# Causal attention: the third output tile of an even step is accumulated in the bank of the widest score tile

## The chip, the cores and the metric

The kernel runs on one core of one Trainium2 chip. Its time is the device time of one launch in microseconds (us). Work is spread over TensorE (PE in the profile, its weight loads PEld), VectorE (DVE), ScalarE (ACT), GpSimd (POOL) and SyncE (SP), which run their own instruction streams and wait for each other on semaphores.

## The reference

Two transformer layers on x of 4 x 512 x 512 (batch, time, width). The change lies in the first layer's attention, run on the layer-normed, modulated h:

```python
q = (x @ wq).reshape(B, T, H, HD)          # H = 32 heads of HD = 128
k, v = x @ wk, x @ wv                      # 8 groups, 4 query heads share one
q, k = rope(q), rope(k)
scores = einsum('bhtd,bhsd->bhts', q, k) / sqrt(HD)
att = softmax(where(causal, scores, -inf))
out = einsum('bhts,bhsd->bhtd', att, v)    # -> B, T, H*HD
return out @ wo                            # (T, 4096) @ (4096, 512)
```

After it come a feed-forward with sign weights, a second attention and a routed low-rank feed-forward; the change does not touch them.

## The kernel before

The batch of 4 is done in two halves of two. In each half `stage_groups` does the attention of the first layer: 64 steps n, one for each of 2 x 32 heads. Two heads make a pair p = n // 2. A float32 product is made of three matmuls on rounded parts (high x high, high x low, low x high), so a 128-row tile with 128 of contraction takes three matmuls.

In step n TensorE does, in this order: transpose the softmaxed scores of head n (`turn`, L713, 4 + 3 tiles), project a key or a value where one is due (`step_e(n, 1)`, L655), make the scores of head n+1 (`scores(n + 1)`, L677), project the query of head n+2 (L655), transpose the last 3 tiles; then in an **even** step three of the four output tiles of the pair before, `out_proj(4(p-1))`, `+1`, `+2` (L758); in an **odd** step probabilities times values, early and late part (`weigh_early`, `weigh_late`, L724), with the fourth tile, `+3`, between them. A key is projected in steps 1, 5, 9, ..., a value in steps 2, 6, 10, ... An output tile is six matmuls of 128 x 512: two heads by three part products. VectorE then adds the tile to a running sum in SBUF (`add`, L1006), and counts `w_added`. The running sum is `y` in the first half and `x` in the second.

PSUM has eight banks of 128 x 512, all taken: `pj` (projections), `pS0`, `pS1`, `pS2` (scores), `pT0`, `pT1` (transposes), `pO` and `pW`. `pS2` holds the widest score tile, of the last 128 rows by 512 keys; it is part 3 of `scores`, done last. VectorE reads the scores in `maxes` (L974), which counts `max_done`, four for each head; once it has read the widest tile, `pS2` is free. In odd steps `pS2` also takes the late half of probabilities times values. Output tiles alternate: first `pW`, second `pO`, third `pW`, fourth `pW`. So the third tile waits until the first has been added.

In an even step VectorE does, after the maxes and the softmax scaling of head n+1: the low part of the last transposes (`pt_los`, L982), the first add, the rounding of the rotated query to its high part (`rope_parts`, L963, which waits for GpSimd's rotation L1143, L1146), the second add, the third add. GpSimd then makes the query's low part `ql` (L1155), which the next step's `scores` needs before its fifth matmul. In the first half, from step 55 on, a piece of the modulation matrices is worked on between the second and the third output tile (`modulate`, L771, L783). After step 63 four more output tiles follow.

Of the kernel before, what the change touches and what calls it, by code (L numbers as in the profile page):

```python
# [27 lines left out]
TT = T // P  # L28
# [474 lines left out]
def stage_groups(nc, held, a, wts, half):  # L503
# [4 lines left out]
    with Stage(nc, f"gqa{half}") as st:  # L508
# [18 lines left out]
        pS = [st.ps(f"pS{i}", [P, T]) for i in range(3)]  # L527
        pT = [st.ps(f"pT{i}", [P, T]) for i in range(2)]
        pO, pW = st.ps("pO", [P, T]), st.ps("pW", [P, D])
# [6 lines left out]
        s_full, max_done, exp_done = st.sem("s_full"), st.sem("max_done"), st.sem("exp_done")  # L536
# [3 lines left out]
        w_full, w_added = st.sem("w_full"), st.sem("w_added")  # L540
# [18 lines left out]
        NTILES = NH // 2 * TT  # L559
# [4 lines left out]
        FIRST_ADDED = NTILES - 2 * TT  # L564

        def wbank(d):
            return pO if d % TT == 1 or d == NTILES - 1 else pW

        def split_no(what, i, group):

            return next(n for n, s in enumerate(SPLIT_LIST) if s[:3] == (what, i, group)) + 1
# [12 lines left out]
        with nc.Block() as block:  # L584
# [39 lines left out]
            def _(pe):  # L624
                def free(e):

                    kind, i = PROJ[e]
                    if kind == "V":
                        pe.wait_ge(v_out, i + 1)
                    else:  # L630
                        pe.wait_ge(cosed, ROPE.index(e) + 1)
# [36 lines left out]
                def scores(n):  # L668
                    u, r = n // R0, n % 2
                    q, k = PROJ.index(("Q", n)), PROJ.index(("K", u))  # L670

                    def part(i, parts):
                        s, c = S_AT[i]
                        t, wide = slice(i * P, (i + 1) * P), max((i + 1) * P, NARROW)
                        for m in parts:
                            qp, kp = ((qh, kh), (qh, kl), (ql, kh))[m]
                            mm = pe.matmul(pS[s][:, c:c + wide], qp[r][:, t], kp[u % 2][:, 0:wide], start=(m == 0), stop=(m == 2))  # L677
                        return mm

                    def drained(s):  # L680
                        if n:
                            pe.wait_ge(max_done, 4 * (n - 1) + S_MAXES[s])

                    pe.wait_ge(rope_hi, ROPE.index(q) + 1)
                    pe.wait_ge(rope_lo, ROPE.index(k) + 1)
                    drained(0)
                    part(1, (0, 1))
                    drained(1)
                    part(0, (0, 1))
                    pe.wait_ge(rope_lo, ROPE.index(q) + 1)  # L690
                    part(1, (2,)).then_inc(s_full, 1)
                    part(0, (2,))
                    part(2, (0, 1, 2)).then_inc(s_full, 1)
                    drained(2)
                    if n >= 3:
                        pe.wait_ge(o_lo, (n - 1) // 2 * 2)
                    part(3, (0, 1, 2)).then_inc(s_full, 1)

                def turn(n, jobs):
# [17 lines left out]
                def weigh(p, out, blocks):  # L717

                    u, m, last = 2 * p // R0, 0, 3 * len(blocks) - 1
                    for j, chunk, at, src, w in blocks:  # L720
                        pe.wait_ge(pt_lo, 3 * (2 * p + 1) + chunk + 1)
                        v = slice(j * P, (j + 1) * P)
                        for vp, pp in ((vh, pth), (vh, ptl), (vl, pth)):
                            mm = pe.matmul(out[:, :, at:at + w], vp[u % 2][:, v], pp[:, :, src:src + w], start=(m == 0), stop=(m == last))  # L724
                            m += 1
                    mm.then_inc(o_full, 1)
# [10 lines left out]
                def weigh_late(p):  # L737

                    pe.wait_ge(max_done, 4 * min(2 * p + 3, NH))
                    weigh(p, late, [(0, 0, 0, PT_OFF[0] + 2 * P, 2 * P), (1, 1, 0, PT_OFF[1] + P, 2 * P),  # L740
                                    (2, 2, 0, PT_OFF[2], 2 * P), (3, 2, P, PT_OFF[3], P)])

                def out_proj(d):

                    pair, i = d // TT, d % TT
                    if d == 0:
                        free(4)
                    if i == 0:
                        pe.wait_ge(o_lo, 2 * pair + 2)
                        pe.wait_ge(w_lo, split_no("o", (2 * pair + 1) % R0, pair // (R0 * HB // 2)))  # L750
                    before = [f for f in range(max(0, d - TT), d) if wbank(f) is wbank(d)]
                    if before:
                        pe.wait_ge(w_added, before[-1] + 1)
                    t = slice(i * P, (i + 1) * P)
                    m = 0
                    for h in (2 * pair, 2 * pair + 1):
                        for op, wp in ((oh, wts.oh), (oh, wts.ol), (ol, wts.oh)):
                            mm = pe.matmul(wbank(d)[:], op[pair % 2][:, h % 2, t], wp[:, h % R0, :], start=(m == 0), stop=(m == 5))  # L758
                            m += 1
                    mm.then_inc(w_full, 1)  # L760
# [25 lines left out]
                for e in range(4):  # L786
                    project(e)
                turn_values(0)
                scores(0)
                for n in range(NH):  # L790
                    if n == 0:
# [6 lines left out]
                    if n + 1 < NH:  # L798
                        scores(n + 1)
# [8 lines left out]
                    p = n // 2  # L808
                    if n % 2 == 0:
                        if p:  # L810
                            out_proj(TT * (p - 1))
                            out_proj(TT * (p - 1) + 1)
                        if later and n >= LATER_AT:
                            modulate(n - LATER_AT)
                        if p:
                            out_proj(TT * (p - 1) + 2)
                    else:
                        weigh_early(p)
                        if p:
                            out_proj(TT * (p - 1) + 3)  # L820
                        weigh_late(p)
                        if later and n >= LATER_AT:
                            modulate(n - LATER_AT)
# [112 lines left out]
            def _(dve):  # L936
# [64 lines left out]
                def add(d):  # L1001
                    dve.wait_ge(w_full, d + 1)
                    if d >= TT:
                        dve.wait_ge(w_added, d - TT + 1)
                    j = (d // (2 * TT)) % HB * TT + d % TT
                    nc.vector.tensor_tensor(y[:, j, :], wbank(d)[:], y[:, j, :], ALU.add).then_inc(w_added, 1)  # L1006
# [1054 lines left out]
```

## Time and profile before

| | us |
|---|---|
| three runs | 2176.83, 2180.11, 2181.4 (median 2180.11) |
| the profiled execution | 2177.08 |
| its span, first to last instruction | 2175.1 |
| mean granted TensorE clock in it | 0.957 of full speed |

The span is 2 us short of the profiled execution's own time. A row of the profile gives a group of instructions by source line, engine and the tiles that it writes and reads; busy time on TensorE is modelled, since its matmuls overlap, so distances between the starts of matmuls tell more than their durations. "Idle before" is the time for which an engine (or TensorE's weight loads, PEld) did nothing ahead of an instruction, with the one that released it.

### The profile page before, as it was taken

Reading aid. Unit: us, or ns where it says so; the run is one execution under the profiler, and the core shown is the slowest. Engines: PE = TensorE matmul, PEld = TensorE weight load, DVE = VectorE, ACT = ScalarE, POOL = GpSimd, SP = SyncE. Lnnn points to the kernel's source line nnn. Section 1 sums busy time; section 2 is a strip of 40 time slices with the busy share of each in tenths; the row PEclk is TensorE's granted clock in tenths of the full one; section 3 lists DMA queues with packets and bytes.
Section 4 is the critical chain, followed back from the end, with each engine's and each line's share of the span. In section 5 each row is a group of like instructions: output and inputs, shape, how many; then the busy total and the mean of one; then the engine's idle time right before and its main releaser. Section 6 shows DMA issues by size and latency. Waiting matters only on the chain. (4 is left out here: it accounts for less than half of the span.)

```text
span 2175.1 us, 33305 instructions
## 1 busy us (share of the span) xinstructions
PE 1987.6 (91%) x11441; PEld 1596.0 (73%) x11441; DVE 1483.2 (68%) x3679; ACT 1067.9 (49%) x2422; POOL 1039.8 (48%) x801
## 2 busy tenths in 40 slices
PE   4899999999999996897948999999999999978797
PEld 3788888888888774475527888888888888745664
DVE  4666676766767666966756767676676667779386
ACT  3555555555555552433235555555555555543232
POOL 3546564645646431544046555555555555417241
PEclk8999999999999997898969999999999999988899
DMA  5000101011010234146321101010110100041561
GB/s 171 20 30 20 30 20 30 20 30 49 20 30 20 78 107 139 64 101 129 85 95 41 30 12 38 20 30 20 30 49 8 42 20 1 30 141 39 116 123 39
DMA packets 132007, 115.30 MB, mean 53 GB/s; under 512 B 43201, under 2 KB 93441, under 8 KB 131841
## 3 DMA queue, kind: packets, MB, share of 16 engines
q1 hardware_dynamic: 124784, 105.51, 16.8%
q10 hardware_dynamic: 7056, 7.68, 1.2%
q8 instruction: 93, 1.52, 0.3%
q14 instruction: 74, 0.60, 0.1%
HBM read 92.15 MB, written 16.81 MB: 50 GB/s over the span
## 5 line engine op out<-in xcount | busy, mean ns | idle before, releaser
L860 ACT ACTIVATE gqa_prob<-gqa_prob,gqa_nmax 128x256 f32<-128x256 f32 (+3 forms) x512 | 284.2, 556 | 154.9 <-DVE gqa_nmax L974 146.6
L870 ACT CAST gqa_pth<-gqa_pT 128x384 fp32r<-128x384 f32 (+1 forms) x384 | 185.5, 519 | 205.3 <-PE gqa_pT L713 202.9
L974 DVE CUSTOM_DVE_ANT_0 gqa_prob<-gqa_pS,consts 128x256 f32<-128x256 f32 (+3 forms) x512 | 222.7, 486 | 58.9 <-PE gqa_pS L677 56.9
L1143 POOL TENSOR_TENSOR x<-x,consts 128x512 f32<-128x512 f32 x80 | 107.3, 1341 | 312.3 <-ACT x L844 312.3
L1143 POOL TENSOR_TENSOR y<-y,consts 128x512 f32<-128x512 f32 x80 | 107.3, 1342 | 303.1 <-ACT y L844 303.1
L982 DVE TENSOR_TENSOR gqa_ptl<-gqa_pT,gqa_pth 128x384 fp32r<-128x384 f32 (+1 forms) x384 | 217.2, 594 | 24.4 <-ACT gqa_pth L870 24.3
L713 PE MATMUL gqa_pT<-consts,gqa_prob 128*128 128x128 f32 x1280 | 183.8, 275 | 20.7 <-DVE gqa_ptl L982 19.2
L655 PE MATMUL gqa_pj<-first_hh,wqh 128*128 128x512 f32 x496 | 195.9, 395 | 0.0
L655 PE MATMUL gqa_pj<-first_hh,wql 128*128 128x512 f32 x496 | 194.7, 393 | 0.0
L655 PE MATMUL gqa_pj<-first_hl,wqh 128*128 128x512 f32 x496 | 194.1, 391 | 0.0
L713 PEld LDWEIGHTS gqa_pT<-consts,gqa_prob 128*128 128x128 f32 x1280 | 154.3, 141 | 48.8 <-DVE gqa_prob L998 15.1
L998 DVE TENSOR_SCALAR gqa_prob<-gqa_prob,gqa_rden 128x128 f32<-128x128 f32 (+3 forms) x512 | 186.4, 427 | 4.6
L758 PE MATMUL gqa_pW<-woh,gqa_oh 128*128 128x512 f32 x380 | 163.3, 430 | 9.7 <-DVE x L1006 5.3
L677 PE MATMUL gqa_pS<-gqa_kh,gqa_qh 128*128 128x256 f32 (+3 forms) x512 | 165.5, 334 | 0.0
L677 PE MATMUL gqa_pS<-gqa_kl,gqa_qh 128*128 128x256 f32 (+3 forms) x512 | 156.6, 324 | 0.0
L758 PE MATMUL gqa_pW<-wol,gqa_oh 128*128 128x512 f32 x380 | 151.0, 397 | 0.0
L758 PE MATMUL gqa_pW<-woh,gqa_ol 128*128 128x512 f32 x380 | 150.8, 397 | 0.0
L677 PE MATMUL gqa_pS<-gqa_kh,gqa_ql 128*128 128x256 f32 (+3 forms) x512 | 144.4, 323 | 1.3 <-POOL gqa_ql L1155 1.3
L655 PE MATMUL gqa_pj<-first_hh,wkvh 128*128 128x512 f32 x248 | 104.2, 420 | 22.3 <-PEq L83 22.3
L994 DVE RECIPROCAL gqa_rden<-gqa_den 128x4 f32<-128x4 f32 x128 | 22.8, 178 | 136.3 <-ACT gqa_prob L860 136.3
L877 ACT CAST gqa_oh<-gqa_pS 128x512 fp32r<-128x512 f32 x64 | 37.5, 586 | 147.3 <-PE gqa_pS L724 147.3
L655 PEld LDWEIGHTS gqa_pj<-first_hh,wqh 128*128 128x128 f32 x496 | 93.2, 188 | 20.6
(333 smaller groups left out, 5284.4 us busy)
## 6 DMA issues: line engine op xcount, KB each, us to landing
raw_o<-in_wo SPq DMA_DIRECT2D x16, 1024.0 KB, 5.2
raw_q<-in_wq SPq DMA_DIRECT2D x14, 1024.0 KB, 5.6
raw_q<-in_wmod SPq DMA_DIRECT2D x10, 1024.0 KB, 5.2
raw_kv<-in_wkv SPq DMA_DIRECT2D x14, 512.0 KB, 6.8
vp<-mid_hf SPq DMA_DIRECT2D x64, 64.0 KB, 1.8
kp<-mid_hf SPq DMA_DIRECT2D x16, 256.0 KB, 2.3
qp<-mid_hf SPq DMA_DIRECT2D x16, 256.0 KB, 2.5
tail_bd<-vp SPq DMA_DIRECT2D x64, 64.0 KB, 3.0
```

Of the source, the lines that this page charges most:

```text
L655: mm = pe.matmul(bank[e][:], wp, hp[:, k, t], start=(n == 0), stop=(n == 3 * KT - 1))
L677: mm = pe.matmul(pS[s][:, c:c + wide], qp[r][:, t], kp[u % 2][:, 0:wide], start=(m == 0), stop=(m == 2))
L713: mm = pe.transpose(pT[k % 2][:, c:c + P], prob[n % 2][:, P_OFF[i] + j * P:P_OFF[i] + (j + 1) * P], held.ident)
L758: mm = pe.matmul(wbank(d)[:], op[pair % 2][:, h % 2, t], wp[:, h % R0, :], start=(m == 0), stop=(m == 5))
L860: ins = nc.scalar.activation(p, p, ACT.Exp, scale=-1.0, bias=nmax[r][:, i:i + 1], accum_out=den[r][:, i:i + 1])
L870: nc.scalar.copy(pth[:, n % 2, c:c + w], pT[k % 2][:, 0:w]).then_inc(pt_hi, 1)
L877: nc.scalar.copy(oh[p % 2][:, :, part * HALF_T:(part + 1) * HALF_T], (early, late)[part]).then_inc(o_hi, 1)
L974: nc.vector.tensor_tensor_reduce(prob[r][:, P_OFF[i]:P_OFF[i] + w], pS[s][:, c:c + w], held.mask[:, T - w:T], -1.0, LARGEST, ALU.add, ALU.min,
L982: nc.vector.tensor_tensor(ptl[:, n % 2, c:c + w], pT[k % 2][:, 0:w], pth[:, n % 2, c:c + w].bitcast(F32), ALU.subtract).then_inc(pt_lo, 1)
L994: nc.vector.reciprocal(rden[n % 2][:], den[n % 2][:]).then_inc(recip, 1)
L998: ins = nc.vector.tensor_scalar(p, p, rden[n % 2][:, i:i + 1], None, ALU.mult)
L1143: nc.gpsimd.tensor_tensor(rot[r % 2][:], rot[r % 2][:], held.sinT, ALU.mult).then_inc(sined, 1)
```

## The change

The third output tile of an even step, all but the last pair's, is accumulated in `pS2` in place of `pW`. Three waits go with it. The tile itself waits for the maxes of the head whose scores last lay in the bank, and no longer for the add of the first tile. The widest score tile of every second head, and the late part of probabilities times values, wait until the tile has been added out of `pS2`.

```diff
         def wbank(d):
-            return pO if d % TT == 1 or d == NTILES - 1 else pW
+            return pO if d % TT == 1 or d == NTILES - 1 else pS[2] if d % TT == 2 and d < NTILES - TT else pW
...
                     drained(2)
                     if n >= 3:
                         pe.wait_ge(o_lo, (n - 1) // 2 * 2)
+                    if n >= 4 and n % 2 == 0:
+                        pe.wait_ge(w_added, TT * (n // 2 - 2) + 3)
                     part(3, (0, 1, 2)).then_inc(s_full, 1)
...
                     pe.wait_ge(max_done, 4 * min(2 * p + 3, NH))
+                    if p:
+                        pe.wait_ge(w_added, TT * (p - 1) + 3)
                     weigh(p, late, [(0, 0, 0, PT_OFF[0] + 2 * P, 2 * P), (1, 1, 0, PT_OFF[1] + P, 2 * P),
...
                     if before:
                         pe.wait_ge(w_added, before[-1] + 1)
+                    if wbank(d) is pS[2]:
+                        pe.wait_ge(max_done, 4 * (2 * pair + 4))
```

The order of instructions is the same on every engine; what moves is the bank, and with it the waits. The listing below names a semaphore by the first name that its number had in the program: here `ln0_mod_summed` is `w_added`, `ln0_ident_in` is `max_done`, `ln0_mod_full` is `o_lo`, `ln0_c_exp` is `pt_lo`. First TensorE at the end of step 4 of the first half, the end of the second output tile and the third, before:

```order
L758 MATMUL gqa0_pO<-woh0,gqa0_oh1 128x512
L758 MATMUL gqa0_pO<-wol0,gqa0_oh1 128x512
L758 MATMUL gqa0_pO<-woh0,gqa0_ol1 128x512
L758 MATMUL gqa0_pW<-woh0,gqa0_oh1 128x512 [waits ln0_mod_summed]
L758 MATMUL gqa0_pW<-wol0,gqa0_oh1 128x512
L758 MATMUL gqa0_pW<-woh0,gqa0_ol1 128x512
```

and the same place in the change:

```order
L764 MATMUL gqa0_pO<-woh0,gqa0_oh1 128x512
L764 MATMUL gqa0_pO<-wol0,gqa0_oh1 128x512
L764 MATMUL gqa0_pO<-woh0,gqa0_ol1 128x512
L764 MATMUL gqa0_pS2<-woh0,gqa0_oh1 128x512 [waits ln0_ident_in,ln0_mod_summed]
L764 MATMUL gqa0_pS2<-wol0,gqa0_oh1 128x512
L764 MATMUL gqa0_pS2<-woh0,gqa0_ol1 128x512
```

The tile goes to another bank. It now waits for the maxes of head 5, and for the add of the third tile of the pair before, which is the last user of `pS2` of its kind; the wait for the first tile of its own pair is gone. Second, TensorE in the step after it, the end of the scores of head 6 with their widest tile, before:

```order
L677 MATMUL gqa0_pS1<-gqa0_kl1,gqa0_qh0 128x384
L677 MATMUL gqa0_pS1<-gqa0_kh1,gqa0_ql0 128x384
L677 MATMUL gqa0_pS2<-gqa0_kh1,gqa0_qh0 128x512 [waits ln0_mod_full,ln0_ident_in]
L677 MATMUL gqa0_pS2<-gqa0_kl1,gqa0_qh0 128x512
L677 MATMUL gqa0_pS2<-gqa0_kh1,gqa0_ql0 128x512
```

and in the change:

```order
L677 MATMUL gqa0_pS1<-gqa0_kl1,gqa0_qh0 128x384
L677 MATMUL gqa0_pS1<-gqa0_kh1,gqa0_ql0 128x384
L677 MATMUL gqa0_pS2<-gqa0_kh1,gqa0_qh0 128x512 [waits ln0_mod_summed,ln0_mod_full,ln0_ident_in]
L677 MATMUL gqa0_pS2<-gqa0_kl1,gqa0_qh0 128x512
L677 MATMUL gqa0_pS2<-gqa0_kh1,gqa0_ql0 128x512
```

The widest tile keeps its two waits and gets a third, for the add of the output tile that was put into its bank.

## Rows read from the trace of the kernel before

**Rows 1.** The page, part 1: busy time and share of the span by engine.
```profile
PE 1987.6 (91%) x11441; PEld 1596.0 (73%) x11441; DVE 1483.2 (68%) x3679; ACT 1067.9 (49%) x2422; POOL 1039.8 (48%) x801
```

**Rows 2.** Busy time by stretch; columns PE, PEld, DVE, ACT, POOL, clock, DMA.
```profile
94.00:720.00 626.00, 623.28 (x3259) 524.31 (x3258) 431.69 (x1140) 353.73 (x852) 341.39 (x264) 1.00 0.08 26
1191.00:1880.00 689.00, 686.09 (x3586) 577.39 (x3585) 476.21 (x1262) 388.38 (x938) 370.36 (x287) 1.00 0.08 25
```

**Rows 3.** Who waited for whom, output tiles only: us, times, longest.
```profile
PEld gqa_pW L758 <- DVE x L1006: 19.1, 32, 2.6
PEld gqa_pW L758 <- DVE y L1006: 14.1, 27, 0.6
PE gqa_pW L758 <- DVE x L1006: 5.3, 16, 2.2
PE gqa_pW L758 <- DVE y L1006: 2.6, 14, 0.2
```

**Rows 4.** Timeline of an even step (n = 28): start, duration, engine, line.
```profile
403.19 0.68 DVE L1006 TENSOR_TENSOR y<-gqa_pW,y 128x512 f32<-128x512 f32 x1
403.30 0.39 PE L758 MATMUL gqa_pO<-wol,gqa_oh 128*128 128x512 f32 x1
...
403.53 0.39 PE L758 MATMUL gqa_pO<-woh,gqa_ol 128*128 128x512 f32 x1
...
403.92 0.19 PEld L758 LDWEIGHTS gqa_pW<-woh,gqa_oh 128*128 128x128 f32 x1 [0.43 <-DVE y L1006]
...
404.26 0.39 PE L758 MATMUL gqa_pW<-wol,gqa_oh 128*128 128x512 f32 x1
```

**Rows 5.** Timeline of the next even step (n = 30), at the third output tile.
```profile
430.12 0.68 DVE L1006 TENSOR_TENSOR y<-gqa_pW,y 128x512 f32<-128x512 f32 x1
...
430.27 0.39 PE L758 MATMUL gqa_pO<-woh,gqa_ol 128*128 128x512 f32 x1
...
430.85 0.19 PEld L758 LDWEIGHTS gqa_pW<-woh,gqa_oh 128*128 128x128 f32 x1 [0.61 <-DVE y L1006]
...
431.19 0.40 PE L758 MATMUL gqa_pW<-wol,gqa_oh 128*128 128x512 f32 x1
```

**Rows 6.** Timeline around that tile: maxes, query's low part, adds, the next scores.
```profile
424.45 0.69 DVE L974 CUSTOM_DVE_ANT_0 gqa_prob<-gqa_pS,consts 128x512 f32<-128x512 f32 x1
...
431.53 0.68 DVE L1006 TENSOR_TENSOR y<-gqa_pO,y 128x512 f32<-128x512 f32 x1
...
431.69 1.29 POOL L1155 TENSOR_TENSOR gqa_ql<-x,gqa_qh 128x512 fp32r<-128x512 f32 x1 [0.54 <-DVE gqa_qh L963]
...
432.54 0.69 DVE L1006 TENSOR_TENSOR y<-gqa_pW,y 128x512 f32<-128x512 f32 x1 [0.33 <-PE gqa_pW L758]
...
433.46 0.30 PEld L677 LDWEIGHTS gqa_pS<-gqa_kh,gqa_ql 128*128 128x128 f32 x2
...
433.98 0.19 PEld L677 LDWEIGHTS gqa_pS<-gqa_kh,gqa_ql 128*128 128x128 f32 x1
434.15 0.19 PEld L677 LDWEIGHTS gqa_pS<-gqa_kh,gqa_qh 128*128 128x128 f32 x1
```

**Rows 7.** Timeline of VectorE right after step 28's third add.
```profile
406.68 0.69 DVE L982 TENSOR_TENSOR gqa_ptl<-gqa_pT,gqa_pth 128x512 fp32r<-128x512 f32 x1 [0.20 <-ACT gqa_pth L870]
```

**Rows 8.** Timeline of step 56 of the first half, with modulation between the tiles.
```profile
738.04 0.68 DVE L1006 TENSOR_TENSOR y<-gqa_pW,y 128x512 f32<-128x512 f32 x1
...
740.59 0.48 PE L758 MATMUL gqa_pW<-woh,gqa_oh 128*128 128x512 f32 x1
```

**Rows 9.** The second half's step 62 and after it: timeline, then one stretch.
```profile
1900.74 0.50 PE L758 MATMUL gqa_pW<-woh,gqa_oh 128*128 128x512 f32 x1 [2.16 <-DVE x L1006]
...
1902.44 0.69 DVE L1006 TENSOR_TENSOR x<-gqa_pW,x 128x512 f32<-128x512 f32 x1 [1.16 <-PE gqa_pW L758]
...
1906.43 0.55 PE L713 MATMUL gqa_pT<-consts,gqa_prob 128*128 128x128 f32 x3 [3.26 <-DVE gqa_ptl L982]
...
1907.00:1911.00 4.00, 4.00 (x13) 3.24 (x13) 3.47 (x6) 1.07 (x2) 0.00 (x0) 0.58 0.01 2
```

## The prediction

> **What bounds the kernel now.** The page's busy shares come first: TensorE is busy 91% of the span, VectorE 68%, the others less [rows 1]. Over the two long stretches of the attention the busy time by stretch sharpens this: 623.28 of 626 us and 686.09 of 689 us on TensorE, at a granted clock of 1.00 (the higher level, 2.4 GHz), against 431.69 and 476.21 us on VectorE [rows 2]. So TensorE bounds these stretches. Whether it has anything to lose must be read from the starts of its matmuls, since their modelled durations overlap.
>
> The view of waits names one wait that comes back all through: output tiles in pW wait for VectorE's add (line 1006), 27 times in the first half (sum in y) and 32 times in the second (sum in x) [rows 3]. The timeline shows it twice. In step 28 matmuls of 512 columns start 0.23 us apart (403.30, 403.53). The next pair of starts should end at 403.99; it ends at 404.26, because the third tile's weights are loaded only at 403.92, 0.05 us after the first tile's add ends at 403.19 + 0.68 = 403.87 [rows 4]. TensorE loses 0.73 - 0.46 = **0.27 us**. In step 30 the add runs from 430.12 to 430.80, the weights come at 430.85, and 430.27 to 431.19 are 0.92 us: **0.46 us** lost [rows 5].
>
> How often each? The weight loads' idle time before the two is 0.43 and 0.61 us [rows 4, 5]. With 13 short and 14 long ones the first half gives 13 x 0.43 + 14 x 0.61 = 14.1 us, which is the row's total. The second half has 15 and 15 of these (15.6 us), one of 2.6 us in step 62, and one at the very end (the last pair's third tile, not moved), which leaves 0.9 us for it [rows 3]. In the first half's last steps modulation lies between the tiles: in step 56 the add ends at 738.72 and the tile starts at 740.59, so nothing is lost there [rows 8].
>
> **The change part by part.** *The wait for the first add goes.* Its replacement is the maxes of head n+1. In step 30 the last of these ends at 424.45 + 0.69 = 425.14, over five microseconds before TensorE wants the bank at about 430.5 [rows 5, 6]. So the third tile starts without a pause.
>
> *Short steps:* 13 + 15 = 28 tiles x 0.27 = 7.6 us. After them comes a key's projection, so the next scores have time. VectorE's part behind it had 0.20 us of idle time before its next transposed tile [rows 7]; TensorE comes 0.27 us earlier, so VectorE is late by some 0.07 us there, with a projection of 12 matmuls (2.7 us) ahead of the next scores to cover it.
>
> *Long steps:* here the next scores follow at once, and what is late next is GpSimd's low part of the query. It ends at 431.69 + 1.29 = 432.98 and its chain began with the query's projection, ahead of the removed pause; it does not move. Its weights were loaded at 433.46 [rows 6]. That is 0.48 us of room, 0.05 us of which a release takes (above), so 0.43 us is left to a tile that comes 0.46 us earlier: a new wait of 0.03 us. Gain 0.43 x 29 = 12.5 us.
>
> *Step 62 of the second half:* TensorE waited 2.16 us for the tile, but VectorE, which leads there, idled only 1.16 us before the third add, and TensorE's next wait is again for VectorE, 3.26 us before 1906.43 [rows 9]. I count VectorE's 1.16 us, rounded to 1.2, and not TensorE's 2.4.
>
> *The added waits.* The next scores' widest tile now waits for the third add. In step 30 that add ends at 432.54 + 0.69 = 433.23 and the widest tile's weights load at 434.15 [rows 6]: 0.92 us of room. After the change the tile's matmuls end 0.46 us earlier; the add must still follow the second, which starts at 431.53 and lasts 0.68, so it ends at 431.53 + 0.68 + 0.69 = 432.90 at the latest, and the weights load at 433.72 (0.43 earlier): 0.8 us of room. Behind this wait on TensorE stand three matmuls, transposes and a query's projection, and VectorE's fourth maximum waits for it. Probabilities times values, late part, come after a whole query projection more: no price. The bare cost of a wait that is already met: before, the widest tile carried two waits and its weights loaded 0.17 us after the load before it (433.98, 434.15), no more than a matmul of 384 columns needs (three quarters of 0.23) [rows 6]. I take zero. The other bound is the 0.05 us of a release for each of some 182 added waits (62 on tiles, 60 on scores, 60 or so on late parts): 9 us.
>
> *Clock.* After 1906.43 the granted clock falls to 0.58 for 1907 to 1911, after pauses of 2.16 and 3.26 us [rows 9]; nine matmuls there took about 0.2 us longer each. The change joins the two pauses to one of some 4.4 us, so the slow stretch stays and may grow by a few matmuls: 0, or up to 2 us lost. I take 0.
>
> **Sum.** 7.6 + 12.5 + 1.2 = 21.3 us, from the profiled execution's own 2177.08: 2155.8 us. That execution was 3 us faster than the median of the three runs, 2180.11, from which the same sum gives 2158.8. I forecast **2157**, between the two.
>
> **Two rules against the rows.** The rows give three readings of one pause: TensorE's matmul row shows 5.3 + 2.6 = 7.9 us of idle time, the weight loads' row 33.2 us [rows 3], and the starts 28 x 0.27 + 29 x 0.46 + 2.4 = 23.3 us. I take the starts: the matmul row counts only what its modelled ends leave, and after a late load the next one follows sooner, so the loads' row counts too much. The Trainium skill (Trainium Kernel Development and Optimization, Performance Expectations) calls matmul busy time a bad measure and the busy share of LDWEIGHTS a good one. By that the change would be worth up to 33.2 us, 2143.9 us; the trace agrees with the first half of it and, with 23.3 us, not with the second as a sum. On the clock the Trainium skill (TensorE: Matmul & The Clock Gate, Part 1) says that a TensorE that goes idle is throttled to half rate; the 0.58 above agrees, and by it the joined pause would cost, not give.
>
> **The rivals.**
> 1. *The gain stops at the next wait* (9%). GpSimd's low part leaves 0.03 us by my rows, but the margin is thin. If it is 0.15 us worse, 29 x 0.15 = 4.4 us are lost: 2160 to 2163 from the two bases. The price of waits at its upper bound, 9 us, ends near it, 2164.8. For it: that chain is the tightest I found. Against: every long step that I read has the same 0.48.
> 2. *Nothing changes* (4%): another engine sets the pace and the pause reappears elsewhere: 2177 to 2180. Against it: VectorE has 30% of the stretch free, the others more [rows 2].
> 3. *Slower* (3%): the widest score tile waits for the third add. It decides once that add ends over 0.8 us later than in the rows; each further tenth costs 60 x 0.1 = 6 us, so a lateness of 1.3 us (two more adds in front of it) would cost 30 us, end at 2177.1 - 21.3 + 30 = 2186. For it: the add is last in VectorE's even step. Against: VectorE idles 0.33 us before it [rows 6].
> 4. *More* (3%): idle loads count in full, 2144; the rows' starts speak against it.
>
> My forecast has the remaining 81%.
>
> **Numbers.** Low end: every pause returned in full, 23.3 us, gives 2153.8; less the 3 us or so by which single runs differ, 2151. High end: rival 1 from the slower base, and the waits' upper bound: 2165. Runs of this kernel differ by 0.2%; within that I call it the same. Faster 0.93 (forecast, rivals 1 and 4), same 0.04, slower 0.03.
>
> **What would show it.** Right: no PEld wait of L764 on the add in an even step before 55; starts 0.23 us apart across the second and third tile; the way from the last matmul of step 28's second tile to that of step 30's (403.53 to 430.27, 26.74 us [rows 4, 5]) shortened to about 26.47; TensorE busy in those stretches unchanged in sum. Wrong: a wait of scores on ql in every fourth step far above 0.03 us; a wait on the add at the widest score tile; a granted clock below 1.00 in the stretch; or the step after 62 slower by more than its 1.2 us.

## The result and the profile after

The changed kernel takes **2156.94 us** (median of four runs, 2156.57 to 2157.57). The kernel before, on the same chip, takes 2179.15 us (median of four, 2176.83 to 2181.4). The ratio is 0.9897, with a 95% interval of 0.9882 to 0.9911: 22.2 us less by the medians. The profiled execution took 2156.57 us, 20.5 us less than the one that the prediction was worked out from.

First the page's busy times, then busy time by stretch (columns as in [rows 2]), of the kernel after:

```profile
PE 1976.0 (92%) x11441; PEld 1605.0 (74%) x11441; DVE 1477.5 (69%) x3679; ACT 1067.6 (50%) x2422; POOL 1040.3 (48%) x801
```
```profile
94.00:710.00 616.00, 616.00 (x3258) 527.07 (x3257) 429.20 (x1140) 353.21 (x851) 341.36 (x264) 1.00 0.09 27
1180.00:1860.00 680.00, 680.00 (x3593) 581.75 (x3592) 474.50 (x1264) 389.15 (x940) 372.03 (x288) 1.00 0.08 25
```

The matmuls, and the instructions of the other engines, are the same in number, and the work of the first stretch now fits into 616 us instead of 626 [rows 2]. TensorE is modelled busy without a gap in both stretches. The same view of before showed only 3 us idle in each [rows 2]; the starts of the matmuls gave the better account.

TensorE's waits for the add of an output tile, all that are left (engine, tile, line, what it waited for: us, times, longest):

```profile
PEld gqa_pW L764 <- DVE x L1012: 0.9, 1, 0.9
PE gqa_pW L764 <- DVE x L1012: 0.5, 1, 0.5
```

Both are of one tile, the last pair's, which was not moved. Of the 59 waits of weight loads in [rows 3], 58 are gone. The timeline of the short step 28 (start, duration, engine, line):

```profile
398.02 0.68 DVE L1012 TENSOR_TENSOR y<-gqa_pW,y 128x512 f32<-128x512 f32 x1
398.13 0.39 PE L764 MATMUL gqa_pO<-wol,gqa_oh 128*128 128x512 f32 x1
...
398.35 0.39 PE L764 MATMUL gqa_pO<-woh,gqa_ol 128*128 128x512 f32 x1
...
398.58 0.39 PE L764 MATMUL gqa_pS<-woh,gqa_oh 128*128 128x512 f32 x1
...
398.81 0.39 PE L764 MATMUL gqa_pS<-wol,gqa_oh 128*128 128x512 f32 x1
...
400.63 0.68 DVE L1012 TENSOR_TENSOR y<-gqa_pS,y 128x512 f32<-128x512 f32 x1
...
401.23 1.14 DVE L988 TENSOR_TENSOR gqa_ptl<-gqa_pT,gqa_pth 128x512 fp32r<-128x512 f32 x2
```

The first tile's add ends at 398.70; the third tile has begun at 398.58 all the same, 0.23 us after the matmul before it. VectorE goes from the third add to the transposed tiles without idle time (no bracket), where it had 0.20 us [rows 7]. The long step 30:

```profile
424.61 0.68 DVE L1012 TENSOR_TENSOR y<-gqa_pW,y 128x512 f32<-128x512 f32 x1
...
424.77 0.39 PE L764 MATMUL gqa_pO<-woh,gqa_ol 128*128 128x512 f32 x1
...
424.99 0.39 PE L764 MATMUL gqa_pS<-woh,gqa_oh 128*128 128x512 f32 x1
...
426.21 1.29 POOL L1161 TENSOR_TENSOR gqa_ql<-x,gqa_qh 128x512 fp32r<-128x512 f32 x1 [0.54 <-DVE gqa_qh L969]
...
426.64 0.68 DVE L1012 TENSOR_TENSOR y<-gqa_pS,y 128x512 f32<-128x512 f32 x1
...
427.36 0.19 PEld L677 LDWEIGHTS gqa_pS<-gqa_kl,gqa_qh 128*128 128x128 f32 x1
...
427.55 0.30 PEld L677 LDWEIGHTS gqa_pS<-gqa_kh,gqa_ql 128*128 128x128 f32 x2
...
428.23 0.19 PEld L677 LDWEIGHTS gqa_pS<-gqa_kh,gqa_qh 128*128 128x128 f32 x1
```

The pause of 0.46 us is gone here too. GpSimd's low part ends at 426.21 + 1.29 = 427.50 and its weights load at 427.55: the 0.48 us of room [rows 6] are used up. Between the second tile's last matmul in step 28 and in step 30 lie 424.77 - 398.35 = 26.42 us, where there were 26.74 and 26.47 were foreseen. The third add ends at 427.32, 0.91 us before the widest score tile's weights load at 428.23.

The end of the second half is the one place with a new long pause. First TensorE's timeline, then busy time by stretch:

```profile
1879.52 0.96 PE L715 MATMUL gqa_pT<-consts,gqa_prob 128*128 128x128 f32 x7 [0.29 <-DVE gqa_ptl L988]
1884.46 0.90 PE L715 MATMUL gqa_pT<-consts,gqa_prob 128*128 128x128 f32 x3 [3.98 <-DVE gqa_ptl L988]
```
```profile
1881.00:1885.00 4.00, 0.54 (x3) 0.54 (x4) 3.93 (x8) 0.15 (x1) 0.00 (x0) 0.75 0.00 0
1885.00:1889.00 4.00, 4.00 (x13) 3.32 (x12) 3.56 (x6) 1.07 (x2) 0.00 (x0) 0.50 0.00 0
```

The two pauses of step 62 and of the step behind it, 2.16 and 3.26 us [rows 9], have become one of 3.98 us, and the granted clock goes to 0.50 in the four microseconds after it (0.58 before): the lower of the two levels, 1.2 GHz.

### The profile page after: what moved, and what is told of

Same layout as the page of the kernel before. It is cut to its first block and busy times, and to the rows that moved or that the text cites. A ratio compares the mean times of both kernels' runs of the same rounds, so it can differ in the third digit from the quotient of the medians.

```text
span 2154.6 us, 33365 instructions
## 1 busy us (share of the span) xinstructions
PE 1976.0 (92%) x11441; PEld 1605.0 (74%) x11441; DVE 1477.5 (69%) x3679; ACT 1067.6 (50%) x2422; POOL 1040.3 (48%) x801
## 5 line engine op out<-in xcount | busy, mean ns | idle before, releaser
L715 PE MATMUL gqa_pT<-consts,gqa_prob 128*128 128x128 f32 x1280 | 184.1, 275 | 21.7 <-DVE gqa_ptl L988 20.2
L764 PE MATMUL gqa_pW<-woh,gqa_oh 128*128 128x512 f32 x256 | 107.5, 420 | 1.9 <-DVE gqa_ol L995 1.4
L655 PEld LDWEIGHTS gqa_pj<-first_hl,wqh 128*128 128x128 f32 x496 | 93.1, 188 | 20.7
L655 PEld LDWEIGHTS gqa_pj<-first_hh,wql 128*128 128x128 f32 x496 | 93.1, 188 | 20.1
```

The source lines that it names most:

```text
L655: mm = pe.matmul(bank[e][:], wp, hp[:, k, t], start=(n == 0), stop=(n == 3 * KT - 1))
L715: mm = pe.transpose(pT[k % 2][:, c:c + P], prob[n % 2][:, P_OFF[i] + j * P:P_OFF[i] + (j + 1) * P], held.ident)
```

## The experiments

The theory: the waits on the first add are the whole matter. Taken away, they give back 0.27 and 0.46 us a tile, less a few hundredths where GpSimd's low part comes next, and the added waits cost nothing. Its rivals: another bank gives something by itself, the gain stops at the next wait, or the widest score tile begins to wait. The kernel before was timed anew beside each group of experiments, and each ratio is taken to its own group: medians of 2177.97 us beside 1 to 4, 2179.15 beside 5 to 8, 2178.74 beside 9 and 10.

To see where the time of an experiment goes I use sums over matmul starts: from the first matmul of output tile 0 to that of tile 104, where the pattern is undisturbed, and from tile 120 to 124 of the second half, the end with step 62. Before: 619.75 and 619.71 us (two halves) and 19.18 us. After: 610.33, 610.32 and 18.85 us. Experiments 7 and 9 do not touch the first of these stretches, and they take 609.91 to 609.98 us there: one profile differs from another by up to 0.4 us.

**1. The other bank, with the old wait.** After, with one wait more at the third tile:

```diff
                         pe.wait_ge(max_done, 4 * (2 * pair + 4))
+                        pe.wait_ge(w_added, d - 1)
```

> The change with one wait more: the third output tile goes to pS2, but still waits for the add of the first tile, which it no longer needs. My theory (the gain is the removed wait and nothing else): back to the time before, 2177 to 2181 us, with pauses of 0.27 and 0.46 us at the third tile. Rival (a tile in another bank is the gain, for instance because tiles of one bank follow each other less closely): stays at 2157.

2181.76 us (ten runs) against 2177.97, ratio 1.0018 [1.0007, 1.0028]. The waits are back, on the new bank:

```profile
PEld gqa_pS L765 <- DVE x L1013: 19.5, 30, 2.6
PEld gqa_pS L765 <- DVE y L1013: 15.2, 26, 0.7
```

So the bank gives nothing; the wait is the whole gain. That it is even 3.8 us slower than before shows in the timeline:

```profile
404.71 0.68 DVE L1013 TENSOR_TENSOR y<-gqa_pW,y 128x512 f32<-128x512 f32 x1
...
405.51 0.19 PEld L765 LDWEIGHTS gqa_pS<-woh,gqa_oh 128*128 128x128 f32 x1 [0.49 <-DVE y L1013]
```

The add ends at 405.39 and the weights load 0.12 us later, where it was 0.05 us [rows 4]. The pauses are 0.34 and 0.52 us (medians over the pattern) instead of 0.28 and 0.46, and 57 x 0.06 = 3.4 us. From tile 0 to tile 120 the two halves are 1.36 and 1.28 us longer than before, so 2.6 us of this stays.

**2 and 3. Short steps alone, long steps alone.** The bank is changed for every second pair; for the short steps as here, for the long ones with `d % (2 * TT) == 2`:

```diff
-            return pO if d % TT == 1 or d == NTILES - 1 else pS[2] if d % TT == 2 and d < NTILES - TT else pW
+            return pO if d % TT == 1 or d == NTILES - 1 else pS[2] if d % (2 * TT) == TT + 2 and d < NTILES - TT else pW
```

> The third tile goes to pS2 only in the short steps (those followed by a key's projection: 28 pauses of 0.27 us), in the long ones to pW as before. My theory: 7.6 us less than before, 2170 to 2172. Rival (a freed pause reappears at the next one, since VectorE paces the steps): no change, 2177 to 2181; or all of the gain, if the pauses of the long steps only follow from those of the short ones: 2157.

> The third tile goes to pS2 only in the long steps (29 pauses of 0.46 us and step 62 of the second half). My theory: 29 x 0.43 = 12.5 us and 0.3 us of step 62 less than before, 2164 to 2167. Rival (the query's low part takes the place of the pause): much less, 2175 and more. The gains of this run and of the short steps' run should add to the whole change's 22 us.

Short alone: 2169.93 us, ratio 0.9963 [0.9948, 0.9977], 8.0 us gained. Long alone: 2165.63 us, 0.9941 [0.9926, 0.9955], 12.3 us gained. The two add up to 20.4 us, against 21.0 for the whole change (2156.94) from the same 2177.97. Neither part pays for the other.

**4. No other bank: the first add sooner.** The kernel before, with VectorE's queue changed: the first add goes ahead of the last transposed tiles' low part (ahead of the values' low part in the long steps), so that the third tile's wait in pW is met in time.

```diff
+                    if p and n % R0 == 0:
+                        add(TT * (p - 1))
                     if not key_step(n):
...
+                    if p and n % R0 == 2:
+                        add(TT * (p - 1))
                     if n % R0 == 2 and n // R0 + 1 < UNITS:
                         value_los(n // R0 + 1)
...
-                    if p:
-                        add(TT * (p - 1) + 3 * (n % 2))
+                    if p and n % 2:
+                        add(TT * (p - 1) + 3)
```

> The kernel before, banks and waits as they were; only VectorE's order is changed: in even steps the first add comes one instruction sooner (ahead of the low part of the last transposes, or ahead of the value's low part). My theory (the pause is VectorE's order, not a lack of banks): the add ends 0.5 to 0.6 us sooner, 403.40 and 430.20 in the places of the profile before, which is just in time for the weights at 403.53 and 430.27; nearly the whole gain, 2157 to 2161. Rival (only another bank removes the pause): 2177 to 2181, or slower because the delayed instruction is waited for.

2156.16 us, ratio 0.9898 [0.9881, 0.9914]: the same gain in the old bank. Its long step:

```profile
424.80 0.68 DVE L1006 TENSOR_TENSOR y<-gqa_pW,y 128x512 f32<-128x512 f32 x1
...
425.56 0.39 PE L758 MATMUL gqa_pO<-woh,gqa_ol 128*128 128x512 f32 x1
425.56 0.19 PEld L758 LDWEIGHTS gqa_pW<-woh,gqa_oh 128*128 128x128 f32 x1
...
425.78 0.39 PE L758 MATMUL gqa_pW<-woh,gqa_oh 128*128 128x512 f32 x1
```

The add is out of the way at 425.48, 0.08 us before TensorE gets to the tile. The Trainium skill (Trainium Kernel Development and Optimization, Best Practices) says that consistent bubbles can mean that SBUF or PSUM has run out. Here the bubble came back every second step, and PSUM was full; but the order of VectorE's queue closes it as well as a bank does.

**5. Rival 3 made real.** After, with the third add moved into the next odd step, behind `pt_los(n, (0, 1))`:

```diff
                     pt_los(n, (0, 1))
+                    if n % 2 and n >= 3:
+                        add(TT * (n // 2 - 1) + 2)
...
-                    if n % 2 == 0 and p:
-                        add(TT * (p - 1) + 2)
```

> The change, but VectorE does the third add only in the next step, after the low parts of that step's first transposes. This uses up the room of the wait that the change puts on the widest score tile. My theory: in the long steps (29) the add ends at about 434.9 on the clock of the profile before, the widest tile wants it at 433.7, so TensorE waits some 1.3 us each time, 38 us in all, less a little that is made up: 2185 to 2205. In the short steps 12 matmuls of a key's projection cover it. Rival (the new wait has so much slack that its place on VectorE does not matter): 2157.

2194.01 us, ratio 1.0069 [1.0053, 1.0084]; 37 us slower than after. TensorE's waits, and one place in the timeline:

```profile
PE gqa_pS L677 <- DVE y L1012: 15.3, 16, 1.0
PE gqa_pS L677 <- DVE x L1012: 14.7, 16, 1.0
```
```profile
438.73 0.68 DVE L1012 TENSOR_TENSOR y<-gqa_pS,y 128x512 f32<-128x512 f32 x1
...
439.53 0.19 PEld L677 LDWEIGHTS gqa_pS<-gqa_kh,gqa_qh 128*128 128x128 f32 x1 [1.24 <-issue]
```

The widest score tile now waits for the add, 32 times, its weights for 1.2 to 1.3 us in nearly all of them. The mechanism is real and dear; what keeps the change clear of it is the 0.91 us of room.

**6. The new wait taken away.** After, with the first matmul of the widest score tile ahead of the wait for GpSimd's low part in every fourth step (`free_wide` makes that tile's three waits):

```diff
+                    ahead = n >= 4 and n % R0 == 0
...
+                    if ahead:
+                        free_wide()
+                        part(3, (0,))
                     pe.wait_ge(rope_lo, ROPE.index(q) + 1)
...
+                    part(3, (1, 2) if ahead else (0, 1, 2)).then_inc(s_full, 1)
```

> The change, and in the scores of every fourth head the first matmul of the widest tile is done ahead of the wait for the query's low part, 0.23 us of work in front of a wait that the profile after shows at 0.05 to 0.07 us. My theory: that wait (29 times) goes, 1.5 to 2 us less than the change, 2154.5 to 2156. Rival (the wait is an artefact of the load's place, the pipeline loses nothing by it): 2157. Second rival: the wide tile now waits for the third add, which leaves it some 0.2 us: slower than 2157.

2153.04 us, ratio 0.9884 [0.9868, 0.9901]. The stretches from tile 0 to 104 take 609.25 us in both halves, 1.08 and 1.07 us less: about 0.08 us a long step. Against 7 and 9, which have the same wait as after, it is about 0.7 us a half, and matmul by matmul that is 0.06 us a long step, all of it at the place itself; the rest of the 1.08 us is the scatter between profiles. So the wait is worth 0.06 us a long step, some 1.7 us for 29 of them, as expected. The remainder of the 3.9 us between the medians lies in stages that this edit does not touch: the time outside the stretches from tile 0 to tile 124 runs from 702.8 to 708.8 us over the profiles.

**7. The pause at the end.** After, with the four `first_residual` of the last steps, which VectorE makes ahead of what TensorE waits for, put off: 0 and 1 into the places of 2 and 3, and these behind `rope_parts` in step 63.

```diff
-                        first_residual(2)
+                        first_residual(0)
...
-                        first_residual(3)
+                        first_residual(1)
...
+                    if n == NH - 1:
+                        first_residual(2)
+                        first_residual(3)
...
-                    if n == NH - 2:
-                        first_residual(0)
-                        first_residual(1)
```

> The change, and at the end of each half VectorE does two of the four residual additions and statistics later, so that the low parts for which TensorE waits (3.98 us in the second half, profile after) come first. My theory: TensorE's pause in step 63 shrinks by some 2.6 us and with it the stretch at the lower granted clock; 2 to 4 us less, 2153 to 2155, of which a part may be given back where VectorE comes late at the stage's end. Rival (VectorE's total at the end of the half leads, its order does not matter): 2157.

2148.61 us, ratio 0.9863 [0.9849, 0.9878]. The same pause, and busy time by stretch around it:

```profile
1879.65 0.55 PE L715 MATMUL gqa_pT<-consts,gqa_prob 128*128 128x128 f32 x3 [1.35 <-DVE gqa_ptl L988]
```
```profile
1878.00:1882.00 4.00, 2.65 (x16) 2.12 (x15) 3.97 (x8) 2.03 (x4) 0.00 (x0) 1.00 0.18 68
1882.00:1886.00 4.00, 3.05 (x15) 2.37 (x13) 3.93 (x7) 0.59 (x1) 0.00 (x0) 1.00 0.01 2
```

1.35 us in place of 3.98, and the granted clock stays at 1.00. In the second half tiles 120 to 123 take 8.39 us instead of 12.20 (11.0 to 14.6 in the other kernels without this edit): 3.8 us gained. To tile 124 it is 14.95 us instead of 18.85: 2.6 us of the pause, 2.5 us because the matmuls behind it take 5.12 us at the granted clock of 1.00 and 7.59 us in after, less 1.2 us by which TensorE waits longer ahead of tile 124. In the first half they take 15.74 instead of 19.29 us, but experiment 10, without this edit, showed 15.62 there once, so that part of the 8.3 us between the medians is not settled.

**8. Both.** Experiments 6 and 7 together.

> The change with the matmul ahead of the wait in every fourth head and the two residuals later. If both gains are real and lie in different stretches they add: 2151.5 to 2154. If one is no gain, this run equals the other one.

2148.84 us, ratio 0.9868 [0.9854, 0.9883]. The gain of 6 is in its stretches (609.33 and 609.25 us), that of 7 in its own (8.39 us again), but in the whole time the gain of 6, under two microseconds, can't be told. The best versions of this study are 7 and 8, some 8 us below the change.

**9. Step 62 not moved.** After, with `d < NTILES - 2 * TT`.

> The change without its last tile of each half (step 62 keeps pW). The profile after shows that this tile gave 0.8 us at step 63 and that 0.5 us of it went again in a longer stretch at the lower granted clock. My theory: within 1 us of the change, 2156 to 2159, and in the profile the stretch from the first tile of step 62 to the first of the last four tiles takes again 19.2 us in the second half as before (18.9 after). My forecast's figure was 1.2 us; were it right, 2158 and 20 us in that stretch.

2159.31 us against 2178.74, ratio 0.991 [0.9895, 0.9924]. TensorE's pauses at the end of the second half:

```profile
1881.27 0.50 PE L764 MATMUL gqa_pW<-woh,gqa_oh 128*128 128x512 f32 x1 [2.16 <-DVE x L1012]
...
1887.17 0.90 PE L715 MATMUL gqa_pT<-consts,gqa_prob 128*128 128x128 f32 x3 [2.53 <-DVE gqa_ptl L988]
```

From tile 120 to 124 it takes 20.39 us, beyond both expectations. My figure for this run, 0.3 us, came from one pair of profiles (19.18 and 18.85), and the ones below show that one pair is not enough. Where step 62's tile is moved and VectorE's end is as in the change, the stretch took 18.85 (after), 18.42 (experiment 3), 17.96 (6) and 17.78 us (10): mean 18.25. Where the wait stays: 19.18 (before), 19.24 (2) and 20.39 us (9): mean 19.60, and 20.50 and 20.36 in 1 and 4, where other things differ as well (4 adds the first tile sooner, but keeps a pause of 2.2 us here): mean of the five 19.93. That is 1.4 to 1.7 us for step 62, with a scatter of some 1 us within each group.

The starts of the matmuls show where that scatter lies. Up to the first of the last three transposes, at which the joined pause ends, the four kernels with the tile moved take 9.58 or 9.59 us, and before, 2 and 9 take 10.83, 10.86 and 11.06 us: 1.2 to 1.5 us. From there to the last matmul of probabilities times values, the stretch with the lower granted clock, the four take 7.59, 7.15, 6.69 and 6.51 us (mean 6.99), the three 6.65, 6.71 and 7.64 us (mean 7.00). So the gain comes ahead of the lower clock, and the longer pause did not make the slow stretch longer on average. My figure falls, and the forecast's 1.2 stands.

**10. The price of a wait that is met.** After, with four waits that are long met ahead of the widest score tile, as here, and in the same way (`d >= TT`) ahead of every output tile but the first four of a half. That makes four waits at 368 places, which the trace counts as 736 more instructions:

```diff
+                    if n >= 4:
+                        pe.wait_ge(rope_hi, 1)
+                        pe.wait_ge(cosed, 1)
+                        pe.wait_ge(v_lo, 1)
+                        pe.wait_ge(o_hi, 1)
```

> The change with 736 more wait instructions on TensorE, all on semaphores that were met long before: ahead of every output tile and of the widest score tile. My theory (a wait that is met costs nothing where TensorE has matmuls in hand): 2156 to 2158. Rival (each costs what a release takes, 0.05 us): 37 us more, 2190 to 2195; the added waits of the change would then have cost it 9 us.

2157.15 us, ratio 0.9901 [0.9884, 0.9917]. The page's first line, of this kernel and (by the same line) of after:

```profile
span 2155.1 us, 34101 instructions
```
```profile
span 2154.6 us, 33365 instructions
```

736 wait instructions more, and the stretches from tile 0 to 104 take 610.15 and 610.26 us against 610.33 and 610.32, a difference inside the 0.4 us of scatter: they cost nothing here.

## Why the prediction was right

It gave 2157 us with a range of 2151 to 2165; the median is 2156.94. Its parts, in its order:

- **What bounds the kernel.** Right: TensorE's matmul starts, and the two pauses read from them. Experiment 1, with the wait put back, brings them back in every step.
- **Short steps, 7.6 us.** Alone they gave 8.0, or 8.3 by the matmul starts up to tile 120 of both halves. VectorE's small lateness behind them was there and was hidden, as said.
- **Long steps, 12.5 us.** Alone they gave 12.3, with step 62 in them; by the matmul starts up to tile 120, and so without step 62, 12.1. The new wait for the low part was put at 0.03 us; followed matmul by matmul through four heads, before against after, the gain of 0.46 us falls to 0.42 there, so it is 0.04. Rival 1, that this wait would be 0.15 us worse, did not come.
- **Step 62, 1.2 us.** 1.2 to 1.5 up to the end of the joined pause (9); I take 1.3. The joined pause of 3.98 us did come (4.4 was foreseen), and the clock was lower behind it, as the term for the clock said it might be. That term was taken as 0, and over four kernels against three it is 0. The lower clock itself costs 1.4 to 2.5 us there, before and after the change, by the 5.12 us of experiment 7 (1.5 us in the profile of before, where the prediction's nine matmuls of 0.2 us make 1.8). In the one pair of profiled executions, the one of after has 0.9 us more of it.
- **Added waits, 0.** Right (10).
- **The widest score tile.** Foreseen with 0.8 us of room; 0.91 measured. Experiment 5 used it up and paid 37 us, about 32 waits of 1.2 us; rival 3 counted 60, but a key's projection covers the tile in the short steps. Rival 3 was a real mechanism that this change stays clear of.
- **The sum.** The stretches up to tile 120 of both halves give back 9.42 + 0.41 + 9.39 + 1.20 = 20.4 us, where the forecast had 7.6 + 12.5 = 20.1. With step 62 that is 21.7 us, against 21.3 foreseen, 22.2 between the medians and 20.5 between the two profiled executions, of which the later one has the longer stretch at the lower clock.

By the idle time of the weight loads, 33.2 us, the kernel would have come to 2143.9. The Trainium skill (Trainium Kernel Development and Optimization, Performance Expectations) calls the busy share of LDWEIGHTS a good measure of how near a kernel is to roofline, which is not the size of a pause. Between the two kernels that share rose from 73% [rows 1] to 74%, by 9 us of busy time, while the time fell by 20.5 us: as a sum neither its idle nor its busy time gives the gain; the starts do.

Two things were luck in part: the forecast lay between two bases 3 us apart, and single executions differ by as much.

## What to carry to other kernels

When a bound engine waits a little for the same thing in every step, measure the pause from the starts of its instructions, count the steps by kind, and look for the next thing due in each kind; here that sum was good to a microsecond in twenty. Before giving such a tile another buffer, see whether the engine that is waited for could do that piece sooner, since a change of its queue gave the same here. A pair of profiles does not settle a term of one microsecond at a place where pauses and the clock vary; several kernels that differ elsewhere can.

## What was not expected of the hardware

- Waits that are met cost TensorE nothing here: 736 more wait instructions moved the stretches by less than 0.2 us.
- The same release took 0.12 us in experiment 1 and 0.05 us before. In before the tile's only wait was on this add; in experiment 1 it has three (two on the same semaphore), and the trace counts 33367 instructions instead of 33305, 62 more. Experiment 5's widest score tile, with three waits, shows the 0.12 us too (the add ends at 439.41, the weights load at 439.53). I take it that a wait in an instruction of its own, ahead of the matmul, passes the release on later; the two forms were not tried apart.
- A pause of 3.98 us was followed by a granted clock of 0.50 over four microseconds; with the pause cut to 1.35 us it stayed at 1.00. One and the same pause had different prices: in after, 3, 6 and 10 it is 3.98 us each time, and the matmuls behind it took 6.51 to 7.59 us, against 5.12 us at 1.00.
